# Normalised rows turned on VectorE and moved through DRAM in a fused graph-attention and mixture-of-experts kernel

## What is computed

```python
h = layernorm(x)
q, k, v = h @ W_q.T + b_q, h @ W_k.T + b_k, h @ W_v.T + b_v
z = (q @ k.T) / sqrt(512) * adj
z = where(z == 0, -10000, z)
x = x + relu(softmax(z, axis=1) @ v)
X = layernorm(x)
r = softmax(X @ Wr)                          # 8 experts
w, i = top_k(r, 2); w = softmax(w)
x = x + swiglu(X, Wg_s, Wu_s, Wd_s) \
      + sum over the two picks e of w[e] * swiglu(X, Wg[e], Wu[e], Wd[e])
# swiglu(X, g, u, d) = (silu(X @ g) * (X @ u)) @ d, inner width 1024
```

## Time and profile before

| what | value |
|---|---|
| runs shown | 1374.38, 1376.58, 1376.89 us |
| profiled execution | 1376.02 us |
| its span, first to last instruction | 1374.4 us |
| mean granted TensorE clock | 0.999 |
| busy: TensorE, VectorE, ScalarE, POOL | 99%, 66%, 33%, 14% |
| chain that ended last | TensorE 89%, DMA 4%, VectorE 3% |
| steps 2 to 13 of attention | 143.96 to 461.60 us |
| first expert matmul | 503.85 us |

### The profile page before, as it was taken

How to read it: one execution, slowest core, us unless ns; L and a number is a source line. 1 busy time by engine, 2 the same in 40 slices (tenths; PEclk the granted TensorE clock), 3 DMA queues, 4 the chain that set the end, 5 groups by cost and what they waited for, 6 DMA issues and landing times.

```text
span 1374.4 us, 19781 instructions
## 1 busy us (share of the span) xinstructions
PE 1365.2 (99%) x6718; PEld 1176.9 (86%) x6718; DVE 902.5 (66%) x1957; ACT 453.7 (33%) x702; POOL 197.8 (14%) x234
## 2 busy tenths in 40 slices
PE   9999999999999999999999999999999999999998
PEld 7888888888888878898989889898898989888887
DVE  7857767767777767465566647566475736367874
ACT  4512212212212244342343324234242525243331
POOL 3500112112211331011011110201102020100000
PEclk9999999999999999999999999999999999999999
DMA  6815665565466663552616143252435262553101
GB/s 188 255 64 151 190 168 158 155 188 164 148 188 179 185 237 138 159 171 55 207 31 215 31 110 121 54 207 36 124 107 152 81 157 97 149 151 108 46 16 62
DMA packets 114420, 185.47 MB, mean 135 GB/s; under 512 B 13776, under 2 KB 47568, under 8 KB 114336
## 3 DMA queue, kind: packets, MB, share of 16 engines
q1 hardware_dynamic: 98064, 153.43, 35.7%
q0 software_dynamic: 9760, 18.93, 7.0%
q10 hardware_dynamic: 6528, 12.22, 3.0%
HBM read 129.82 MB, written 55.77 MB: 135 GB/s over the span
## 4 chain that ended last, share of the span: by engine, by line
PE 89%; DMA 4%; DVE 3%; issue 2%; ACT 1%; SPq 1%; DVEq 0%; ACTq 0%
PE bank L307 81%; PE bank L1043 5%; DMA p_moved<-turned 2%; DMA turned<-p_moved 2%; PE bank L1034 1%; PE bank L875 1%; ACT sc L1211 1%; PE bank L799 1%; DVE fill L1608 0%; DMA early_x<-x2t 0%; DVE pT_l L1458 0%; DVE turned L1626 0%; SPq L460 0%; PE bank L869 0%; DMA wq_raw<-in_L_gnn_W_q_dram 0%
## 5 line engine op out<-in xcount | busy, mean ns | idle before, releaser
L1852 DVE TENSOR_TENSOR hid<-bank,hid 128x384 f32<-128x384 f32 (+1 forms) x80 | 46.8, 585 | 176.8 <-PE bank L307 176.5
L307 PE MATMUL bank<-dn_h,hT_h 128*128 128x512 f32 x320 | 125.8, 393 | 0.2 <-DVE hT_l L1458 0.2
L307 PE MATMUL bank<-dn_h,hT_l 128*128 128x512 f32 x320 | 125.7, 393 | 0.0
L307 PE MATMUL bank<-dn_l,hT_h 128*128 128x512 f32 x320 | 125.5, 392 | 0.0
L307 PE MATMUL bank<-xq_h,gate_h 128*128 128x384 f32 (+1 forms) x320 | 111.3, 348 | 0.1
L307 PE MATMUL bank<-xq_h,gate_l 128*128 128x384 f32 (+1 forms) x320 | 111.2, 347 | 0.0
L307 PE MATMUL bank<-xq_l,gate_h 128*128 128x384 f32 (+1 forms) x320 | 110.9, 346 | 0.0
L307 PE MATMUL bank<-xq_h,up_h 128*128 128x384 f32 (+1 forms) x320 | 110.7, 346 | 0.0
L307 PE MATMUL bank<-xq_h,up_l 128*128 128x384 f32 (+1 forms) x320 | 110.5, 345 | 0.0
L307 PE MATMUL bank<-xq_l,up_h 128*128 128x384 f32 (+1 forms) x320 | 110.4, 345 | 0.0
L1129 ACT ACTIVATE hT_h<-hid 128x384 fp32r<-128x384 f32 (+1 forms) x96 | 53.8, 561 | 164.3 <-DVE hid L1852 124.7
(11 more groups left out here) (278 smaller groups left out, 3287.8 us busy)
## 6 DMA issues: line engine op xcount, KB each, us to landing
gate_raw<-in_L_ffn_Wg_dram SPq DMA_DIRECT2D x16, 1024.0 KB, 5.4
up_raw<-in_L_ffn_Wu_dram SPq DMA_DIRECT2D x16, 1024.0 KB, 9.4
dn_raw<-in_L_ffn_Wd_dram SPq DMA_DIRECT2D x16, 1024.0 KB, 12.3
sc<-in_adj_dram SPq DMA_DIRECT2D x30, 512.0 KB, 6.2
p_moved<-turned SPq DMA_DIRECT2D x30, 512.0 KB, 3.0
turned<-p_moved SPq DMA_DIRECT2D x120, 128.0 KB, 5.4
x_t<-in_x_dram SPq DMA_DIRECT2D x24, 256.0 KB, 4.9
slots<-x2row ACTq DMA_DIRECT2D x12, 512.0 KB, 4.3
```

The costliest lines, as they stand in the source:

```text
L307: mm = pe.matmul(o, lhs(a, c), rhs(b, c), start=first and n == 1, stop=last and n == 3 * len(chunks))
L1852: dve.tensor_tensor(hid[:, c % 2, 0:w], bank[2 + c % 2][:, 0:w], hid[:, c % 2, 0:w], ALU.mult).then_inc(sem("hid"), 1)
```

## The change

- `turn_normalised` and `keep_turned` are left in steps 14 and 15 and for the last row tile. In steps 1 to 13 VectorE turns the row's squares (`turn_row`, one transpose of 128x512 from x2row to `x2_squares`), SP stores them to DRAM and reads them back in four loads (`move_rows`), and ScalarE copies the result to x2T (`join_turned`). `x2_squares` and `x2_banks` lie where x2T and x1 lie, so `turn_row` waits for the logits and the store of x2T of the step before, the loads wait for the store of x1, and `output` waits for x2T.
- `store` is cut in two. In the loop x2T is stored by `store_turned` within `move`, ahead of the eight loads.
- `route_logits` goes behind attend 1 in odd steps and behind attend 2 in even ones. VectorE's `logits` go behind the second y_f in even steps, ahead of the last `queries_low`, and `picks` behind that.
- `count_picks` goes behind the scores' second bank, `take_counts` behind the masks (in odd steps also behind `low(i, 0)`, which goes ahead of `ranks`).
- Step 14 takes the picks ahead of the first tokens and leaves one of their two pieces to step 15. In step 15 the counts go behind the first attention group and `turn(2)`.
- At the kernel's end eight stores share one semaphore.

```diff
@@ -59,6 +59,8 @@
     p_moved = nc.dram_tensor("p_moved", [2, P, BANKS * HALF * Q], F32, kind="Internal").ap()
+    x2_moved = nc.dram_tensor("x2_moved", [P, BANKS * D // BANKS], F32, kind="Internal").ap()
     x2t = nc.dram_tensor("x2t", [T, DC * P], F32, kind="Internal").ap()
@@ -91,6 +93,10 @@
 x2T = at("x2T", 194 * K, [P, DC, P])
+x2_squares = at("x2_squares", 194 * K, [P, BANKS, DC, Q])
+x2_banks = at("x2_banks", 192 * K, [P, BANKS, DC, Q])
 x2row = [at("x2row0", 196 * K, [P, D]), at("x2row1", 200 * K, [P, D])]
@@ -261,6 +267,8 @@
 LAST_O = bank[3]
+ROWS = NT - 3
 TURNED = 2 * (NT - 1)
@@ -444,7 +452,7 @@
         sp.dma_start(x_t[:, b, :], rows(x, i)).then_inc(sem(f"xr_in{b}"), 16)
-    def move(i):
+    def move(i, stored=False):
@@ -453,24 +461,43 @@
                 load_adj(i + 1, h)
+        if stored:
+            store_turned(i - 2)
         for h in range(2):
...
                 sp.dma_start(turned[Q * a:Q * a + Q, h, :, :], by_bank[a]).then_inc(sem(f"p_half{h}"), 16)
+    def move_rows(i):
+        sp.wait_ge(sem("row_turned"), i + 1)
+        sp.dma_start(x2_moved, x2_squares[:].rearrange("p a c q -> p (a c q)")).then_inc(sem("row_moved"), 16)
+        sp.wait_ge(sem("x1_out"), 16 * (i + 1))
+        sp.wait_ge(sem("row_moved"), MOVED * i + 16)
+        by_bank = x2_moved.rearrange("(i r) (a f) -> a r i f", i=BANKS, a=BANKS)
+        for a in range(BANKS):
+            sp.dma_start(x2_banks[Q * a:Q * a + Q, :, :, :].rearrange("p i c q -> p i (c q)"), by_bank[a]
+                         ).then_inc(sem("row_moved"), 16)
     def store(i):
...
         sp.dma_start(rows(acc, i), x1[:]).then_inc(sem("x1_out"), 16)
+    def store_turned(i):
         sp.wait_ge(sem("x2T_done"), i + 1)
...
         fetch(i, b)
-        if not isinstance(i, int) or i > 0:
+        stored = not isinstance(i, int) or i > 0
+        if stored:
             store(i - 1)
-        move(i + 1)
+            move_rows(i - 1)
+        move(i + 1, stored)
     move(0)
@@ -480,6 +507,7 @@
     store(NT - 3)
+    store_turned(NT - 3)
     def load_turned(o, b, name):
@@ -519,12 +547,14 @@
     store(NT - 2)
+    store_turned(NT - 2)
     sp.wait_ge(sem("attended"), 4 * NT)
...
     store(NT - 1)
+    store_turned(NT - 1)
     sp.wait_ge(sem("sent"), 64 * NT)
@@ -617,11 +647,9 @@
             sp.wait_ge(sem("z_done"), 4 + 4 * n + k + 1)
-            sp.dma_start(rows(out, 8 + 4 * n + k), z[:, n, k, :]).then_inc(sem(f"out{n + 1}"), 16)
-    sp.wait_ge(sem("out"), 16)
+            sp.dma_start(rows(out, 8 + 4 * n + k), z[:, n, k, :]).then_inc(sem("out"), 16)
+    sp.wait_ge(sem("out"), 16 + 2 * 64)
     sp.wait_ge(sem("out0"), 64)
-    sp.wait_ge(sem("out1"), 64)
-    sp.wait_ge(sem("out2"), 64)
 @block.gpsimd
@@ -871,6 +899,7 @@
         wait(pe, "x2T_done", i)
+        wait(pe, "counts_read", i - 1)
         for c in range(DC):
@@ -886,9 +915,9 @@
         if last:
-            count_picks(i - 1)
             attend(i, 0, last)
             turn(2)
+            count_picks(i - 1)
             attend(i, 1, last)
@@ -899,21 +928,25 @@
         scores(i + 1, 1 - b, 0)
+        scores(i + 1, 1 - b, 1)
         if prev and not (isinstance(i, int) and i == 1):
             count_picks(i - 1)
-        scores(i + 1, 1 - b, 1)
         scores(i + 1, 1 - b, 2)
-        if prev:
+        if split:
             turn_normalised(i, b)
         scores(i + 1, 1 - b, 3)
-        if prev:
+        if split:
             route_logits(i)
...
         attend(i, 1)
+        if prev and b == 1:
+            route_logits(i)
         attend(i, 2)
+        if prev and b == 0 and not split:
+            route_logits(i)
         if split:
@@ -1222,8 +1255,12 @@
         copy(pT["h"][:, 4 * g:4 * g + 4, :].rearrange("p k q -> p (k q)"), bank[4 + g % 2][:]).then_inc(sem("pT_h"), 1)
+    def join_turned(i):
+        wait(act, "row_moved", MOVED * i)
+        copy(x2T[:].rearrange("p c (i q) -> p i c q", q=Q), x2_banks[:]).then_inc(sem("x2T_done"), 1)
     def keep_turned(i):
-        wait(act, "x2_turned", i)
+        wait(act, "x2_turned", i - ROWS)
         wait(act, "logits", i - 1)
@@ -1241,7 +1278,7 @@
             last_group(1)
-            first_pieces(2, 3)
+            first_pieces(1, 3)
             last_group(2)
@@ -1250,18 +1287,26 @@
         high(i, 0)
+        if split:
+            keep_turned(i)
         high(i, 1)
-        if prev:
-            keep_turned(i)
+        short = b == 1 or split
+        if prev and b == 1:
+            join_turned(i)
         probabilities(i + 1, 1 - b)
-        if prev:
+        if prev and short:
             router_exp(i)
+        if prev and not short:
+            join_turned(i)
         if split:
-            first_pieces(0, 2)
+            first_pieces(0, 1)
         if queries_follow(j, b):
...
         if prev:
+            if not short:
+                router_exp(i)
             pick_exp(i)
@@ -1321,7 +1366,7 @@
             if b < 2:
-                act.wait_ge(sem("x2_turned"), NT + q + 1)
+                act.wait_ge(sem("x2_turned"), NT - ROWS + q + 1)
                 copy(o[:, :, part], bank[(c + 1) % 2 if b == 0 else 7][:].rearrange("p (c q) -> p c q", c=DC)).then_inc(sem("xq_h"), 1)
@@ -1646,6 +1691,8 @@
         wait(dve, "x2_done", i - 1)
+        wait(dve, "x2T_done", min(i - 1, ROWS) if isinstance(i, int) else i - 1)
         wait(dve, "rden_done", i)
@@ -1661,8 +1708,19 @@
     def row_normalised(i, b):
-        wait(dve, "x2_turned", i - 2)
+        if isinstance(i, int) and i - 2 > ROWS:
+            dve.wait_ge(sem("x2_turned"), i - 2 - ROWS)
+        else:
+            wait(dve, "row_turned", i - 2)
         normalise(x2row[1 - b][:], x1[:], NT + i, 1 - b).then_inc(sem("x2_done"), 1)
+    def turn_row(i, b):
+        wait(dve, "x2_done", i)
+        wait(dve, "logits", i - 1)
+        wait(dve, "x2t_out", 16 * (i - 1))
+        dve.transpose(x2_squares[:], x2row[1 - b][:].rearrange("p (c a q) -> p a c q", a=BANKS, q=Q)
+                      ).then_inc(sem("row_turned"), 1)
     def logits(i):
@@ -1721,14 +1779,14 @@
             output(i, b)
+            residual(i, b, j + b)
             take_counts(i - 1)
+            row_normalised(i, b)
+            last_group(2)
             ranks(i - 1)
-            residual(i, b, j + b)
-            last_group(2)
-            row_normalised(i, b)
+            first_pieces(1, 2)
             last_group(3)
-            first_pieces(2, 3)
-            first_pieces(3, 4)
+            first_pieces(2, 4)
             logits(i)
@@ -1738,9 +1796,9 @@
             residual(i, b, j + b)
-            if counted:
-                take_counts(i - 1)
             row_normalised(i, b)
+            if not split:
+                turn_row(i, b)
         if not prev:
@@ -1763,11 +1821,16 @@
             return
+        if b == 1:
+            low(i, 0)
         if counted:
+            take_counts(i - 1)
             ranks(i - 1)
         fill_zeros(i + 1, 1 - b, 0)
-        low(i, 0)
+        if b == 0:
+            low(i, 0)
         fill_zeros(i + 1, 1 - b, 1)
@@ -1775,21 +1838,25 @@
         row_max(i + 1, 1 - b)
-        if prev:
+        short = b == 1 or split
+        if prev and short:
             logits(i)
...
         if split:
-            first_pieces(0, 2)
+            picks(i)
+            first_pieces(0, 1)
         else:
...
             scaled_queries(2 * j + 3, 1)
-        if prev:
-            picks(i)
+        if prev and not short:
+            logits(i)
         if ahead:
             queries_low(2 * j + 3, 1)
+        if prev and not split:
+            picks(i)
         if prev:
...
```

## The result

The changed kernel takes 1379.53 us (median of 10 runs, 1378.81 to 1380.50). The kernel before took 1375.24 in ten runs on the same chip (1374.38 to 1376.92). The ratio is 1.0030, 95% interval 1.0021 to 1.0039: slower by 4.3 us, and the interval, 0.2 to 0.4%, doesn't reach down to no change. The profiled execution took 1380.41 us, one of the longer of the ten; its span is 1378.8.

The account below looks back on a forecast made before the run. TensorE bound the loop (52.61 us a pair against VectorE's 51.08); the change makes VectorE the bound at 53.9. With the end's gains the first expert matmul comes 0.9 later: 1376.02 + 0.9 = 1376.9 us, range 1371 to 1382.5.

Parts of the forecast that it names:

- The loop: Attention loop: VectorE's path per pair (even plus odd step) grows from 51.08 to 53.9 us, becoming the bound.
- turn and wait: VectorE, each loop step: turn_row's transpose 0.62 us plus 0.2 for its wait on x2_done, together 0.82.
- The counts: VectorE, each loop step: take_counts behind the masks loses its cover in the power's pause and costs 0.2 us.
- TensorE's own path: TensorE in the loop: without turn_normalised its pair falls by 0.88 us, from 52.61 to 51.73.
- the 2.0 us for waits on x2T: TensorE, three longer even steps: logits waiting for x2T take some 2.0 us in all, which can go.
- The attribution of the 0.8: VectorE, even steps: later logits cost 0.39 us unhidden, and queries_low waits 0.4 more for ScalarE's yT_h, so 0.8.
- The step that failed: Step 14's x1 to last_group(0): 24.46 us becomes 20.8, as the early tokens' wait goes and other waits and work come.
- The rival of a falling clock: Loop: TensorE's waits drop its clock, two or three such falls costing 3 to 5 us: 1381 us, chance 0.10.
- The end: Last step: 14.91 us becomes 13.3 without the lower clock, 13.5 with the counts; nothing changes behind it.
- Hidden altogether: Loop: VectorE's additions are hidden, TensorE stays the bound and pockets the savings: 1363 to 1367 us, chance 0.07.
- cheap: Loop: VectorE's additions take their lower bounds, the pair is 52.9 us, five pairs save 5: 1372 us, chance 0.14.
- Late probabilities: Loop, odd steps' low(i, 0): turned probabilities load late behind the x2t store; 2.2 us delay gives 1382 us, chance 0.15.

Follow-up runs that it names:

- experiment 2: The kernel after, with a second, equal transpose behind the first in turn_row: 1386.50 us, ratio 1.0083 to the kernel before.
- experiment 5: The kernel after, with take_counts back in the power's pause (behind residual) in every step: 1375.10 us, ratio 0.9997 to the kernel before.
- Experiment 7: experiment 6 without its move of the picks, which stay behind the last queries_low in even steps: 1375.24 us, ratio 1.0004 to the kernel before.
- Experiment 8: experiment 6 with take_counts moved behind the masks and low(i, 0) in odd steps: 1371.46 us, ratio 0.9969 to the kernel before.
- experiment 1: The kernel after, with take_counts put ahead of row_normalised in step 14 alone: 1377.61 us, ratio 1.0020 to the kernel before.
- experiment 6: experiment 5 with even steps' logits in the exponential's pause, join ahead of it, route_logits behind attend 0, picks ahead of the last queries_low: 1379.90 us, ratio 1.0040.
- experiment 4: The kernel before with only the reordered end, the edits of steps 14 and 15: 1371.95 us, ratio 0.9980.
- experiment 9: The kernel before, rows still turned on TensorE, with the later logits and the reordered end together: 1371.79 us, ratio 0.9975.

## Why the prediction held in its range and was low by 2.6 us

The 2.6 us flatter it. The change was forecast to cost 0.9 us and cost 4.3, so 3.4 were missed. The forecast started from the profiled execution of 1376.02, and the ten runs of the kernel before have a median of 1375.24: the start was 0.8 too high, which by luck hid a part of the miss. At the first expert matmul, where the two traces compare directly, 3.1 are missing (507.82 against 504.7).

**The loop: right, term by term.** The bound did pass to VectorE. From x2row to the first mask it is 313.58 - 312.36 = 1.22 us, where the earlier trace rows show 0.46 to the next instruction: 0.76 a step for turn and wait, against 0.82 (the turn itself is 313.58 - 312.94 = 0.64, against 0.62). The counts cost 315.06 - 314.86 = 0.20, as priced. The rest of the even step's growth is 28.12 - 26.39 - 0.76 - 0.20 = 0.77, against 0.8. In experiment 2 a doubled turn lengthens the pair by 1.43, nearly its own 2 x 0.75, and in experiment 5 the counts shorten it by 2 x 0.22: what VectorE is given or spared shows nearly in full. TensorE's own path was right too: steps 2 and 3, where it waits for nothing, take 28.74 + 22.96 = 51.70, against 51.73. Only the 2.0 us for waits on x2T were read too high, from the lengths of the steps: the waits view has 1.1. The sum did not use them.

**The attribution of the 0.8: wrong in part.** The prediction split it into 0.39 for the logits and 0.4 for waiting. Experiment 7 shows one wait for ScalarE's answer, which the logits only fill: it is 1.57 us from y_f to `yT_l` with them or without. Experiment 8 shows what does remove the 0.8: even steps of 27.12 instead of 28.12, of which 0.2 are the counts and 0.8 the picks' place.

**The step that failed: from x1 of step 14 to `last_group(0)`, put at 20.8 us.** I priced there the early tokens' wait, a piece and the counts on VectorE, and followed the late counts on VectorE alone. The other side was left out: the written-out step 14 keeps `turn_normalised`, and that waits on `counts_read` for bank 7. TensorE's matmuls had ended and x2row was written by 474.17, but the copy of the counts came at 475.40, and TensorE stood for 3.02 us in all. The late counts were followed to `ranks` on VectorE, not to TensorE. VectorE itself lost only the copy's 0.2 by them up to the exponential: from x1 to `row_max` it takes 14.62 us (470.17 to 484.79), and 14.41 in experiment 1 (470.41 to 484.82). Experiment 1 moves the counts alone; the wait falls to 1.55, and the landmarks come to 0.6 us from the forecast's.

**The clock.** The rival of a falling clock was placed in the loop. There five odd steps wait, up to 1.15 us each, and the clock stays at 1.00 (it did fall in the loops of experiments 6 and 7). It fell in step 14 instead, behind the 3.02 us. From 475.71 to 481.68 the four transposes and twelve matmuls take 5.97 us, where experiment 1 takes 3.32 (474.46 to 477.78): 2.65 for the clock. With the longer wait the attention products start 3.6 us later than there (482.49 against 478.92), and step 15 still 2.6, as experiment 1 waits 0.69 for pT_l at that point and the kernel after doesn't.

**The end: right.** The last step takes 13.52 against 13.5, and no wait is left in it. The sum of the change, at the first expert matmul, is then: x1 of step 14 is 6.43 us late, step 14 adds 2.5 that experiment 1 takes away, and the total is 3.97 late. So the reordered end gives some 5 back; this is the remainder, not a measurement, and experiment 4 measures 4.2 on the kernel before. Behind it the span takes 870.98 us against 870.55.

**The other rivals.** Hidden altogether, or cheap: no, the pair is 53.94 and not 52.9. Late probabilities: ScalarE has the first half of pT_h in step 9 at 340.49 + 1.06 and VectorE comes to `low(i, 0)` at 342.9. The store of x2t ahead of their loads costs VectorE nothing, and the loads' median is 5.5 us instead of 5.4.

**The two rules of the Trainium skill.** By the Trainium skill's drain (VectorE: DVE Perf Modes, The DRAIN you can't avoid) the wait on x2_done would have been free. Here the next instruction starts 0.58 us after x2row with the wait and 0.46 without: it costs 0.12, between the page's nothing and my 0.2. The same section of the Trainium skill says that a next operation which is not held starts earlier, and the 0.46, shorter than x2row's own 0.55, agrees; the prediction had left this out. The Trainium skill's advice to give a 128x128 transpose to TensorE (VectorE: DVE Perf Modes, Rules for kernel authors) holds for the change as made. With the same end, the later logits and the counts back, rows on VectorE took 1375.10 us (experiment 5) and rows on TensorE 1371.79 (experiment 9, on the same chip). With picks and counts rearranged (experiment 8) the two come level.

## What to carry to other kernels

When an engine with a low mean share has a chain through the loop, add up its own path from one fixed instruction to the same one a period later, pauses included: it forecast this loop's pair to 0.1 us. For each instruction that is moved back, list everyone who waits for its semaphore, in the written-out first and last steps too. What an instruction costs depends on whether it stands where the engine waits for an answer anyway: one that fills such a gap is free, and the gap is what is paid when it leaves.

## What was not expected of the hardware

- The lower clock comes at different distances behind a wait. After: 3.02 us idle, and already the four transposes are slow (1.09 us), then the matmuls at 0.63 to 481.3. Experiment 2, with 3.08 us idle at the same place, still has its transposes and two matmuls at the upper level, and 0.63 from 484.28 to 487.24, TensorE's timeline:

```profile
484.05 0.41 PE L315 MATMUL bank<-xnT_l,yT_h 128*128 128x512 f32 x1
484.28 0.60 PE L315 MATMUL bank<-xnT_h,yT_l 128*128 128x512 f32 x1
...
487.24 0.61 PE L315 MATMUL bank<-xnT_h,yT_h 128*128 128x512 f32 x1
```

  Shorter waits can bring it too, and the same wait brings it once and not another time. Of experiment 6's five waits of 2.06 to 2.09 us before odd steps only the last is followed by it (eight matmuls, 443.32 to 446.26); of experiment 7's six waits for x2T only the last of the loop, of 1.17 us, is. The two of 1.47 and 0.74 us close together in the earlier trace rows brought it as well. Single waits of 1.55 us (experiment 1) and 1.32 (experiment 5), and those of up to 1.15 in the kernel after, did not. What sets the moment was not tried.
- The turned row is long on its way in even steps. SP issues the store at 313.68 and the loads at 318.39, since it also waits for the x1 store that was issued just before; in the odd step it is 341.73 and 344.58. SP's timeline of the kernel after, and its waits from 300 to 360 us (total, times, longest):

```profile
312.80 0.36 SPq L487 DMA_DIRECT2D acc<-x  x1
313.68 0.32 SPq L476 DMA_DIRECT2D x_moved<-x_squares  x1
318.39 1.84 SPq L481 DMA_DIRECT2D x_banks<-x_moved  x4
...
341.73 0.32 SPq L476 DMA_DIRECT2D x_moved<-x_squares  x1
344.58 1.75 SPq L481 DMA_DIRECT2D x_banks<-x_moved  x4
```
```profile
SPq L478 <- DMA acc<-x: 1.8, 1, 1.8
```

  From the turn's start to the end of the copy into x2T it is 7.5 us in the odd step (340.99 to 348.52) and, in experiment 8, where ScalarE takes the row at once, 11.4 in the even one (309.39 to 320.80); the prediction had 8 to 9 for both. It harms nothing in the kernel after, as x2T is taken behind the exponential there anyway.
